# Cross-attention and mixture of experts on one core: the queries and keys stacked from SBUF to SBUF, the start of the kernel in four pieces, and 20 transposes of the identity

## The chip, the cores and the metric

The kernel is one program on one NeuronCore of a Trainium2 chip. The time is that of the device in microseconds; the kernel before took 1139.05 us (median of 3 runs, 1137.99 to 1144.78).

## The reference, cut to what matters

The input is `x` (8 batches of 256 tokens, 512 features) and a context of the same shape. One layer is computed, in float32:

```
x = x + attention(layernorm(x), ctx)      # 32 query heads of 16, 8 key/value groups
x = x + experts(layernorm(x))             # top 4 of 32 experts, a large and a small one each
```

```
qh = q @ Wq.T ;  kh = ctx @ Wk.T ;  vh = ctx @ Wv.T
score = qh @ kh / sqrt(16) ;  attn = softmax(score) ;  out = (attn @ vh) @ Wfc.T + bfc
```

Four heads share one group of keys and values. The change touches the attention alone; routing and the experts stay as they are.

## The kernel before, in words

The attention runs batch by batch (`b` of 8) and, within a batch, in 16 **steps** (`j`), each of two heads. A score is wanted at float32 accuracy from bf16 matmuls, so each of `q` and `k` is split into three bf16 parts (high, middle, low; ACT, DVE and POOL make one each: `q_first`, `q_split`, `q_third`, lines 229 to 405). The parts are then **stacked** over 96 partitions, so that one matmul with 96 rows gives the six products that count: `qst` holds high three times, middle twice, low once, `kst` the matching partners. Two more rows (96 and 97) hold the negative row maximum, so that the second score matmul gives score minus maximum.

The stacking moves data between partitions and is done by DMAs of the SP queue. Before, they go by DRAM: `store_q` writes `q3` to `qd` (L140), and `stack_q` reads it back in three DMAs of 48, 32 and 16 partitions (L151). The same holds for `k` (L157, and six DMAs of 16 partitions, L169). `stack_max` (L184) sends the two rows of maxima of one **chunk** (4 steps, 8 heads) in two DMAs.

Each step on TensorE is, in this order (L750 to L759):

```
scores(b, j)            # stp: 4 matmuls with 98 rows, exp on ACT follows; at j = 0, 4, 8, 12 waits for the chunk's maxima
side_items(b, j)        # one slice of other work: projections, transposes, the output product
scores_for_max(b1, j1)  # s: 4 matmuls with 96 rows for the step LEAD steps ahead, row maxima on DVE follow
values(b, g)            # ov: only in even steps, the products with v
```

`LEAD` is 9: the maxima run nine steps ahead. A chunk of maxima is turned by `transpose_max` (L573, out tile `turn`), which waits until DVE has reduced the chunk's last heads; `split_max` (L419) makes two bf16 parts; `stack_max` sends them. `transpose_max` stands in steps 3, 7, 11 and 15, behind a slice of other side work. As it turns the chunk that step j-1 completed, two of these steps later its scores are asked for.

The SP queue's order in batch b is: stack k and q of batch b+1 (they wait for the last scores of batch b-1, because the buffers alternate), the context of b+2, then the maxima of the chunks, and the stores of b+2. Chunk 1 of a batch is turned in step 15 of the batch before, so its DMAs are issued ahead of the stacking.

Before the loop there is a **start**: load `x`, context and weights; moments, rsqrt by ACT `Sqrt` and DVE reciprocal, normalise; project k, v, q of batch 0, then of batch 1 (L715 to L737); then nine steps of maxima of batch 0 (L739 to L746); then the loop.

Of the kernel before, what the change touches and what calls it, by code (L numbers as in the profile page):

```python
# [14 lines left out]
P = 128  # L15
# [13 lines left out]
RUNS = ((0, 3), (1, 2), (2, 1))  # L29
ROWS_QK = DH * sum(n for _, n in RUNS)  # L30
ROWS_ST = ROWS_QK + 2
LEAD = 9
CH = 4
# [5 lines left out]
def attention(nc, x_in, ctx_in, wq, wk, wv, wfc, bfc, xs, st_new, ident, qd, kd):  # L39
# [3 lines left out]
    with ExitStack() as ctx:  # L43
# [7 lines left out]
        ctxT = sb("ctxT", [P, C, S], F32)  # L51
# [3 lines left out]
        std, rstd = sb("std", [P, NT], F32), sb("rstd", [P, NT], F32)  # L55
        xn = sb("xn", [P, TT, D], F32)
        xnT = sb("xnT", [P, C, S], F32)
        q3 = sb("q3", [P, 3, C * S], BF16)
# [21 lines left out]
        kvw_loaded, wq_loaded = sem("kvw_loaded"), sem("wq_loaded")  # L80

        GROUPS = ((0, 2), (2, 4), (4, 10), (10, 16))
        x_loaded = [sem(f"x_loaded{n}") for n in range(len(GROUPS))]
        c_loaded = sem("c_loaded")
        ident_ready, set_up = sem("ident_ready"), sem("set_up")
        stats, var_ready, std_ready, rstd_ready = sem("stats"), sem("var_ready"), sem("std_ready"), sem("rstd_ready")
# [11 lines left out]
        q_stored, k_stored, q_stacked, k_stacked = sem("q_stored"), sem("k_stored"), sem("q_stacked"), sem("k_stacked")  # L98
# [4 lines left out]
        def q_parts(n):  # L103

            return [q3[:, l, n * 512:(n + 1) * 512] for l in range(3)]
# [12 lines left out]
        def _(sp):  # L118
# [6 lines left out]
            def load_ctx(b):  # L125
                sp.dma_start(ctxT[:, :, :], ctx_in[b]).then_inc(c_loaded, DMA)
# [3 lines left out]
            sp.dma_start(Wk[:, :, :], wk).then_inc(kvw_loaded, DMA)  # L130
            sp.dma_start(Wv[:, :, :], wv).then_inc(kvw_loaded, DMA)
            sp.dma_start(Wq[:, :, :], wq).then_inc(wq_loaded, DMA)
            for k in range(1, len(GROUPS)):
                load_x(k)
            sp.dma_start(Wfc[:, :, :], wfc).then_inc(w_loaded, DMA)
            sp.dma_start(Bfc[:, :], bfc).then_inc(w_loaded, DMA)

            def store_q(b):
                sp.wait_ge(q_lo, b * 2 + 2)
                sp.dma_start(qd[b].rearrange("l p n -> p l n"), q3[:, :, :]).then_inc(q_stored, DMA)  # L140

            def stack_q(b):

                sp.wait_ge(q_stored, b * DMA + DMA)
                if b >= 2:
                    sp.wait_ge(st_ready, (b - 1) * H)
                src = qd[b].rearrange("l (d g) n -> (l d) (g n)", g=G)
                at = 0
                for l, n in RUNS:
                    dst = qst[b % 2][at:at + n * DH, :, :].rearrange("p h t -> p (h t)")  # L150
                    sp.dma_start(dst, src[0:n * DH, :]).then_inc(q_stacked, DMA)  # L151
                    at += n * DH

            def store_k(b):

                sp.wait_ge(k_lo, b + 1)
                sp.dma_start(kd[b].rearrange("l p n -> p l n"), k3[b % 2][:, :, :]).then_inc(k_stored, DMA)  # L157

            def stack_k(b):

                sp.wait_ge(k_stored, b * DMA + DMA)
                if b >= 2:
                    sp.wait_ge(st_ready, (b - 1) * H)
                src = kd[b].rearrange("l (d g) n -> l d (g n)", g=G)
                at = 0
                for l, n in RUNS:
                    for _ in range(n):
                        dst = kst[b % 2][at:at + DH, :, :].rearrange("p g t -> p (g t)")
                        sp.dma_start(dst, src[l]).then_inc(k_stacked, DMA)  # L169
                        at += DH  # L170

            def next_ctx(b):
                if b < NB:
                    sp.wait_ge(v_full, b)
                    load_ctx(b)

            def stack_max(n):

                b, c = n // NC, n % NC
                sp.wait_ge(mt_empty, n + 1)  # L180
                heads = slice(c * 2 * CH, (c + 1) * 2 * CH)
                for l in range(2):
                    dst = qst[b % 2][ROWS_QK + l:ROWS_QK + l + 1, heads, :].rearrange("o h t -> o (h t)")
                    sp.dma_start(dst, nm[n % 2][:, l, :])\  # L184
                      .then_inc(m_ready[n % 2], DMA)

            sp.wait_ge(set_up, 1)
            store_k(0)
            next_ctx(1)
            stack_k(0)  # L190
            store_q(0)
            stack_q(0)
            store_k(1)
            stack_k(1)
            store_q(1)
            stack_q(1)
            for n in range(LEAD // CH):
                stack_max(n)

            for b in range(NB):  # L200
                if 0 < b < NB - 1:
                    stack_k(b + 1)
                    stack_q(b + 1)
                next_ctx(b + 2)
                for j in range(3, J, CH):
                    if chunk_at(b, j) < NB * NC:
                        stack_max(chunk_at(b, j))
                    if j == 11 and b < NB - 2:
                        store_q(b + 2)
                        store_k(b + 2)  # L210

        @block.gpsimd
        def _(pool):
# [4 lines left out]

            def add_bias(b):
# [5 lines left out]

            def q_third(b, n):

                pool.wait_ge(q_mid, b * 2 + n + 1)
                pool.tensor_tensor(q_parts(n)[2], qres[n][:, :], q_parts(n)[1], ALU.subtract).then_inc(q_lo, 1)  # L229
# [7 lines left out]
            q_third(0, 0)  # L237
            q_third(0, 1)
# [4 lines left out]
            for b in range(3):  # L243
                add_bias(b)
            for b in range(NB):
                if b < NB - 2:
                    q_third(b + 2, 0)
                if b < NB - 3:
                    add_bias(b + 3)
                if b < NB - 2:  # L250
# [4 lines left out]
        def _(act):  # L255
            def deviations(k):
                t0, t1 = GROUPS[k]
                act.wait_ge(var_ready, k + 1)
                act.activation(std[:, t0:t1], mv[:, t0:t1, 1], ACT.Sqrt, bias=eps[:, :]).then_inc(std_ready, 1)
# [5 lines left out]
            def k_first(b):  # L265
                act.wait_ge(k_full, b + 1)
                if b >= 2:
                    act.wait_ge(k_stored, (b - 1) * DMA)
                act.copy(k3[b % 2][:, 0, :], turn[:, 0:S]).then_inc(k_hi, 1)

            def v_evac(b):

                act.wait_ge(v_full, b + 1)
                if b == 0:
                    act.wait_ge(set_up, 1)
# [4 lines left out]

            def q_first(b, n):
                if n == 0 and b:
                    act.wait_ge(q_stored, b * DMA)
                act.wait_ge(qp_full, b * 2 + n + 1)
                act.copy(q_parts(n)[0], side[:, :]).then_inc(q_hi, 1)
# [25 lines left out]

            deviations(0)
            k_first(0)
            v_evac(0)
            deviations(1)
            x_evac(0, 0)
            x_evac(0, 1)
            q_first(0, 0)
            q_first(0, 1)
            deviations(2)  # L320
            deviations(3)
# [4 lines left out]
            q_first(1, 1)  # L326

            for b in range(NB):
                for j in range(J):
                    exponentials(b, j)  # L330
                    if j == 0 and b < NB - 2:
                        x_evac(b + 2, 0)
                    if j == 1 and b:
                        ov_evac(b - 1, 3)
                    if j == 1 and b < NB - 2:
                        x_evac(b + 2, 1)
                    if j == 1 and b < NB - 1:
                        v_evac(b + 1)
                    if j == 4 and b:
                        o_evac(b - 1, 0)  # L340
                    if j == 4 and b < NB - 2:
# [3 lines left out]
                    if j == 5 and b:  # L345
                        o_evac(b - 1, 1)
                    if j == 11 and b < NB - 2:
                        q_first(b + 2, 1)
                    if j == 12 and b < NB - 2:
# [6 lines left out]
        def _(dve):  # L356
            dve.memset(eps[:, :], EPS)
            for i in range(2):
                dve.memset(mx[i][:, :], 0.0)
                dve.memset(vx[i][:, :, :, DH:VW], 1.0)  # L360
                m = dve.memset(kst[i][ROWS_QK:P, :, :], 1.0)
            m.then_inc(set_up, 1)

            def moments(k):

                dve.wait_ge(x_loaded[k], DMA)
                for t in range(*GROUPS[k]):
                    dve.bn_stats(st6[:, t, :], xs[:, t, :]).then_inc(stats, 1)
                for t in range(*GROUPS[k]):
# [4 lines left out]
            def invert(k):  # L374

                t0, t1 = GROUPS[k]
                dve.wait_ge(std_ready, k + 1)
                dve.reciprocal(rstd[:, t0:t1], std[:, t0:t1]).then_inc(rstd_ready, 1)
                dve.wait_ge(rstd_ready, k + 1)
# [17 lines left out]

            def q_split(b, n):

                dve.wait_ge(q_hi, b * 2 + n + 1)  # L400
                if b:
                    dve.wait_ge(q_lo, b * 2 + n - 1)
                dve.tensor_tensor(qres[n][:, :], side[:, :], q_parts(n)[0], ALU.subtract).then_inc(qp_empty, 1)  # L403
                dve.wait_ge(qp_empty, b * 2 + n + 1)
                dve.tensor_copy(q_parts(n)[1], qres[n][:, :]).then_inc(q_mid, 1)  # L405

            def row_max(b, j):
                for r in range(2):
                    h = 2 * (j % CH) + r
                    dve.wait_ge(s1_ready, b * H + 2 * j + r + 1)  # L410
                    dve.tensor_reduce(mx[j // CH % 2][:, 2 * h:2 * h + 2], s1[r][:, :, :], AX.X, ALU.max)\  # L411
                       .then_inc(max_done, 1)

            def split_max(n):

                dve.wait_ge(mt_full, n + 1)
                if n >= 2:
                    dve.wait_ge(m_ready[n % 2], n // 2 * 2 * DMA)
# [5 lines left out]
            def weigh(b, p):  # L424
# [8 lines left out]
                dst = o[b % 2][:, :, p * P:(p + 1) * P].rearrange("p t (k d) -> p t k d", d=DH)  # L433
# [13 lines left out]
            invert(0)  # L447
# [962 lines left out]
```

## Time and profile before

| | before |
|---|---|
| median of 3 runs | 1139.05 us |
| profiled execution, its own time | 1136.86 us |
| its span | 1135.1 us |
| TensorE busy in the span | 1026.3 us, 90% |
| VectorE busy | 423.1 us, 37% |
| ScalarE busy | 347.1 us, 31% |
| GpSimd busy | 292.9 us, 26% |
| first score matmul for the exponentials | 68.18 us |

The profile page gives busy time per engine, the span in 40 slices, the DMA queues, the chain that ended last and the costliest groups. The loop of the attention runs from about 68 to 430 us, routing to about 500 us, the experts to the end.

### The profile page before, as it was taken

To read this page: it belongs to the slowest core of one execution; us is meant where nothing else is said; L and a number is where in the kernel's file an instruction comes from. 1 tells how busy PE (TensorE), PEld (TensorE's weight loads), DVE (VectorE), ACT (ScalarE), POOL (GpSimd) and SP (SyncE) were. 2 spreads that over 40 slices of the span, in tenths; PEclk is the share of its full clock that TensorE was granted. 3 is DMA by queue.
4 is the path that set the end of the run, shared out by engine and by line. 5 is a ranking of instruction groups with operands and counts; after the bars stand their busy time and mean duration, and the time that the engine had idled before them with its cause. 6 is when DMAs were issued, how large, how long until landed. Compare 5 with 4: busy or idle time off the path is not lost.

```text
span 1135.1 us, 18843 instructions
## 1 busy us (share of the span) xinstructions
PE 1026.3 (90%) x5498; PEld 660.9 (58%) x5500; DVE 423.1 (37%) x1019; ACT 347.1 (31%) x630; POOL 292.9 (26%) x381
## 2 busy tenths in 40 slices
PE   5589999999999988427999999999999999999995
PEld 4356666666655536315666666666666666666662
DVE  5457667666667624691111111111111111111110
ACT  1135544555545533141222222222222222222221
POOL 1211101101000000202344334334334343433442
PEclk9779999999999998757999999999999999999998
DMA  8531451422513003931755776675665767667433
GB/s 307 136 72 48 79 122 39 90 75 52 125 36 71 3 1 133 366 115 42 222 148 141 217 220 146 213 224 144 190 171 150 207 181 199 198 153 221 76 65 48
DMA packets 44120, 154.51 MB, mean 136 GB/s; under 512 B 9136, under 2 KB 12336, under 8 KB 38960
## 3 DMA queue, kind: packets, MB, share of 16 engines
q1 hardware_dynamic: 26448, 111.23, 31.0%
q0 software_dynamic: 17632, 42.74, 19.2%
q8 instruction: 26, 0.43, 0.2%
q14 instruction: 14, 0.11, 0.0%
HBM read 116.46 MB, written 37.22 MB: 135 GB/s over the span
## 4 chain that ended last, share of the span: by engine, by line
PE 53%; issue 1%; DMA 0%; ACT 0%; DVEq 0%; POOL 0%; DVE 0%; POOLq 0%; ACTq 0%
PE y_ps L1324 18%; PE g_ps L1307 15%; PE u_ps L1307 15%; PE xt_ps L1300 3%; PE at_ps L1316 2%; DMA xg<-xd,gidx 0%; POOL out_x L1211 0%; DVEq L1288 0%; ACT sg L1236 0%; ACT yb L1243 0%; ACT xT L1232 0%; DVE aT L1265 0%; DVEq L1289 0%; DVE a L1278 0%; DVE a L1279 0%
## 5 line engine op out<-in xcount | busy, mean ns | idle before, releaser
L1324 PE MATMUL y_ps<-W,aT 128*128 x468 | 215.5, 597 | 2.5 <-DVE aT L1265 2.5
L1211 POOL DMA_INDIRECT out_x<-yb,yidx x78 | 125.3, 1606 | 298.0 <-DMA out_x<-yb,yidx 134.7
L309 ACT ACTIVATE pt<-stp 128x512 f32<-128x512 f32 x256 | 139.0, 596 | 173.2 <-PE stp L556 172.2
L411 DVE TENSOR_REDUCE mx<-s 128x2 f32<-128x512 f32 x256 | 164.0, 682 | 69.4 <-PE s L542 68.0
L1307 PE MATMUL g_ps<-W,xT 128*128 x624 | 183.3, 437 | 0.9 <-ACT xT L1232 0.9
L1307 PE MATMUL u_ps<-W,xT 128*128 x624 | 181.3, 433 | 0.0
L1307 PEld LDWEIGHTS u_ps<-W,xT 128*128 128x128 f32 x624 | 119.1, 191 | 49.9 <-issue 0.8
L1307 PEld LDWEIGHTS g_ps<-W,xT 128*128 128x128 f32 x624 | 113.5, 192 | 39.0 <-issue 2.4
L1278 DVE TENSOR_TENSOR a<-u_ps,sg 128x192 f32<-128x192 f32 x78 | 27.9, 358 | 287.6 <-ACT sg L1236 287.6
L1324 PEld LDWEIGHTS y_ps<-W,aT 128*128 128x128 f32 x468 | 83.5, 192 | 78.3 <-issue 78.3
L1236 ACT ACTIVATE sg<-g_ps 128x320 f32<-128x320 f32 x78 | 34.1, 437 | 305.5 <-PE u_ps L1307 305.5
L1265 DVE COPY aT<-at_ps 128x384 f32<-128x384 f32 x78 | 43.5, 558 | 183.1 <-PE at_ps L1316 176.9
L1243 ACT ACTIVATE yb<-y_ps,wt 128x512 f32<-128x512 f32 x78 | 53.6, 687 | 168.5 <-PE y_ps L1324 156.0
L1197 POOL DMA_INDIRECT xg<-xd,gidx x80 | 80.7, 1008 | 69.4 <-POOL gidx L1194 65.4
L542 PE MATMUL s<-kst,qst 96*128 96x256 bf16 x512 | 83.9, 282 | 7.5 <-DVE mx L411 7.4
L556 PE MATMUL stp<-qst,kst 98*128 98x256 bf16 x512 | 78.4, 276 | 2.8 <-DMA qst<-nm 2.3
L229 POOL TENSOR_TENSOR q<-qres,q 128x512 bf16<-128x512 f32 x16 | 19.0, 1188 | 236.5 <-DVE q L405 236.5
L542 PEld LDWEIGHTS s<-kst,qst 96*128 96x128 bf16 x512 | 48.2, 99 | 49.4 <-DVE mx L411 22.9
L514 PE MATMUL side<-xnT,Wq 128*128 128x256 f32 x256 | 66.5, 394 | 5.8 <-DVE qres L403 2.9
L1194 POOL COPY gidx<-tok 128x1 uint32 (+1 forms) x80 | 58.5, 731 | 40.1 <-POOLq L799 29.6
L569 PE MATMUL ov<-pt,vx 128*32 128x256 f32 x1024 | 68.5, 385 | 0.2
L556 PEld LDWEIGHTS stp<-qst,kst 98*128 98x128 bf16 x512 | 44.6, 98 | 35.7 <-issue 28.9
(155 smaller groups left out, 932.2 us busy)
## 6 DMA issues: line engine op xcount, KB each, us to landing
W<-in_wts SPq DMA_DIRECT2D x32, 2048.0 KB, 8.4
qd<-q SPq DMA_DIRECT2D x8, 768.0 KB, 3.6
qst<-qd SPq DMA_DIRECT2D x8, 768.0 KB, 7.5
ctxT<-in_ctx SPq DMA_DIRECT2D x8, 512.0 KB, 11.6
qst<-qd SPq DMA_DIRECT2D x8, 512.0 KB, 10.1
xd<-r_xn SPq DMA_DIRECT2D x16, 256.0 KB, 2.0
out_x<-xs SPq DMA_DIRECT2D x1, 4096.0 KB, 13.9
xs<-in_x SPq DMA_DIRECT2D x2, 1536.0 KB, 13.6
```

What stands on the lines that cost most here:

```text
L309: act.activation(pt[g % 2][:, 2 * (j % 2) + r, :, :], stp[n % STP][:, :, :], ACT.Exp, scale=DH ** -0.5).then_inc(exp_done, 1)
L411: dve.tensor_reduce(mx[j // CH % 2][:, 2 * h:2 * h + 2], s1[r][:, :, :], AX.X, ALU.max)\
L514: m = pe.matmul(side[:, k * S:(k + 1) * S], Wq[:, c, (2 * n + k) * P:(2 * n + k + 1) * P], xnT[:, c, :], start=(c == 0), stop=(c == C - 1))
L542: m = pe.matmul(s1[r][:, t, :], qst[b % 2][0:ROWS_QK, 2 * j + r, t * P:(t + 1) * P], kst[b % 2][0:ROWS_QK, j // 2, :], start=True, stop=True)
L556: m = pe.matmul(stp[n % STP][:, t, :], kst[b % 2][0:ROWS_ST, j // 2, t * P:(t + 1) * P], qst[b % 2][0:ROWS_ST, 2 * j + r, :], start=True, ...
L569: m = pe.matmul(ov[c * VW:(c + 1) * VW, g % 2, :], vx[b % 2][:, t, g, :], pt[(b * G + g) % 2][:, c, t, :], start=(t == 0), stop=(t == TT - 1))
L1194: pool.tensor_copy(idx[p][:, :], tok[:, bass.ds(s, 1)]).then_inc(idx_ready, 1)
L1197: pool.indirect_dma_start(xg[p][:, :], None, xd[:, :], bass.IndirectOffsetOnAxis(idx[p][:, :], 0))\
L1211: pool.indirect_dma_start(out[:, :], bass.IndirectOffsetOnAxis(yidx[p][:, :], 0), yb[p][:, :], None, compute_op=ALU.add).then_inc(y_added, ...
L1243: act.activation(yb[p][:, :], y_ps[:, :], ACT.Copy, scale=wt[p][:, :]).then_inc(y_empty, 1)
L1307: m = pe.matmul(ps_[p][:, 0:IW], xT[p][:, c, :], W[:, bass.ds(buf, 1), (2 * c + g) * IW:(2 * c + g + 1) * IW] .rearrange("p a f -> p (a f) ...
L1324: m = pe.matmul(y_ps[:, :], aT[p][:, c, :], W[:, bass.ds(buf, 1), GW + c * D:GW + (c + 1) * D].rearrange("p a d -> p (a d)"), start=(c == ...
```

## The change

- `store_q`, `store_k` and the DRAM tensors go. `stack_q` and `stack_k` copy from SBUF to SBUF, six DMAs each, every one to 16 partitions. `q3` and `ctxT` get a second buffer.
- Batch 0's q is projected, split and stacked in four chunks (`project_q0`, `q0_first`, `q0_split`, `q0_third`, `stack_q0`), each in a PSUM tile of its own. The heads are taken in another order (`head`), so that a chunk of the projection is a chunk of four steps.
- `LEAD` is 8. `transpose_max` stands first among the side items of steps 0, 4, 8 and 12, and every other side item moves one step later. The start's maxima of batch 0 run among the projections of batch 1.
- `stack_max` takes four DMAs a chunk; in each batch chunk 1 now comes behind the stacking and the context on the SP queue.
- The moments of batches 2 to 7 are made batch by batch, in the loop from batch 3 on; rsqrt is exp(-0.5 ln) on ACT plus one Newton step (three small DVE instructions).
- Twenty transposes of the identity run on TensorE ahead of its first wait for weights.

```diff
-RUNS = ((0, 3), (1, 2), (2, 1))
+ROWS_OF_Q = ((0, 16, 32), (48, 64), (80,))
+ROWS_OF_K = ((0, 48, 80), (16, 64), (32,))
-LEAD = 9
+LEAD = 8
...
             load_x(0)
             load_ctx(0)
+            sp.dma_start(Wk[:, :, :], wk).then_inc(wk_loaded, DMA)
             sp.dma_start(Wq[:, :, :], wq).then_inc(wq_loaded, DMA)
+            sp.dma_start(Wv[:, :, :], wv).then_inc(wv_loaded, DMA)
+            load_x(1)
+            load_ctx(1)
...
+            def stack_q0(c):
+                for n, ready in ((0, q0_hi), (1, q0_mid), (2, q0_lo)):
+                    sp.wait_ge(ready, c + 1)
+                    for at in ROWS_OF_Q[n]:
+                        dst = qst[0][at:at + DH, c::C, :]
+                        sp.dma_start(dst, q0_parts(c)[n]).then_inc(q0_stacked[c], DMA)
+            def stack_q(b):
+                if b >= 2:
+                    sp.wait_ge(st_ready, (b - 1) * H)
+                for n, ready in ((0, q_hi), (1, q_mid), (2, q_lo)):
+                    sp.wait_ge(ready, q_counts(b, 1) + 1)
+                    for at in ROWS_OF_Q[n]:
+                        dst = qst[b % 2][at:at + DH, :, :].rearrange("p h t -> p (h t)")
+                        sp.dma_start(dst, q3[b % 2][:, n, :]).then_inc(q_stacked, DMA)
...
             def stack_max(n):
                 b, c = n // NC, n % NC
                 sp.wait_ge(mt_empty, n + 1)
                 for l in range(2):
+                    for t in range(TT):
+                        dst = qst[b % 2][ROWS_QK + l:ROWS_QK + l + 1, c::C, t * P:(t + 1) * P]
+                        sp.dma_start(dst, nm[n % 2][t * G:(t + 1) * G, l, :]).then_inc(m_ready[n % 2], DMA)
+            stack_k(0)
+            stack_q0(0)
+            load_x(2)
+            for c in range(1, C):
+                stack_q0(c)
             sp.dma_start(Wfc[:, :, :], wfc).then_inc(w_loaded, DMA)
             sp.dma_start(Bfc[:, :], bfc).then_inc(w_loaded, DMA)
+            load_x(3)
+            stack_max(0)
             stack_k(1)
             stack_q(1)
             for b in range(NB):
                 if 0 < b < NB - 1:
                     stack_k(b + 1)
                     stack_q(b + 1)
                 next_ctx(b + 2)
-                for j in range(3, J, CH):
+                for j in range(0, J, CH):
                     if chunk_at(b, j) < NB * NC:
                         stack_max(chunk_at(b, j))
...
             # VectorE, the start
             moments(0)
-            invert(0)
+            refine(0)
             normalise(0, 0)
             normalise(0, 1)
             k_split(0)
+            for c in range(C):
+                q0_split(c)
             moments(1)
+            refine(1)
             normalise(1, 0)
             normalise(1, 1)
+            for j in range(LEAD):
+                if j == 1:
+                    k_split(1)
+                if j == 4:
+                    split_max(0)
+                    q_split(1, 0)
+                if j == 5:
+                    moments(2)
+                if j == 7:
+                    q_split(1, 1)
+                row_max(0, j)
+            refine(2)
             normalise(2, 0)
             normalise(2, 1)
             for b in range(NB):
                 for j in range(J):
                     if j == 0 and b >= 2:
                         add_out(b - 2, 1)
+                    if j % CH == 0 and chunk_at(b, j) < NB * NC:
+                        split_max(chunk_at(b, j))
-                    if j == 2 and b:
+                    if j == 3 and b:
                         weigh(b - 1, 3)
+                    if j == 4 and b < NB - 3:
+                        moments(b + 3)
-                    if j == 5 and b < NB - 2:
+                    if j == 6 and b < NB - 2:
                         q_split(b + 2, 0)
-                    if j in (6, 10, 14):
+                    if j in (7, 11, 15):
                         weigh(b, j // 4 - 1)
-                    if j == 9 and b:
+                    if j == 10 and b:
                         add_out(b - 1, 0)
...
             # TensorE
+                if j % CH == 0 and chunk_at(b, j) < NB * NC:
+                    ...
+                    transpose_max(chunk_at(b, j))
-                if j == 5 and b:
+                if j == 6 and b:
                     pe.wait_ge(ot_empty, (b - 1) * TT + 1)
                     transpose_o(b - 1, 1)
                     if b < NB - 2:
-                        pe.wait_ge(qp_empty, (b + 2) * 2 + 1)
+                        pe.wait_ge(qp_empty, q_counts(b + 2, 0) + 1)
                     project_out(b - 1, 0, (0,))
-                if j == 9 and b < NB - 2:
+                if j == 10 and b < NB - 2:
                     if b:
                         pe.wait_ge(fc_empty, (b - 1) * TT + 1)
                     project_q(b + 2, 1, (0, 1, 2))
...
+            pe.wait_ge(ident_ready, 2)
+            for _ in range(20):
+                pe.transpose(turn[:, 0:P], ident[:, :], ident[:, :])
+            pe.wait_ge(wk_loaded, DMA)
             project_k(0)
+            transpose_x0(0)
+            transpose_x0(1)
+            pe.wait_ge(wq_loaded, DMA)
+            pe.wait_ge(xt_empty, TT)
+            for k in range(C):
+                project_q0(k)
+            pe.wait_ge(wv_loaded, DMA)
             project_v(0, 0)
             project_v(0, 1)
             project_k(1)
+            for j in range(LEAD):
+                scores_for_max(0, j)
+                if j == 0:
+                    transpose_x(1, 0)
+                if j == 1:
+                    transpose_x(1, 1)
+                if j == 2:
+                    project_q(1, 0, range(C))
+                if j == 3:
+                    project_q(1, 0, range(C, 2 * C))
+                    transpose_max(0)
+                if j == 5:
+                    project_q(1, 1, range(C))
+                if j == 6:
+                    project_q(1, 1, range(C, 2 * C))
```

## Rows read from the trace of the kernel before

**Rows 1.** The page's first part: busy time, share of the span, instructions.

```profile
PE 1026.3 (90%) x5498; PEld 660.9 (58%) x5500; DVE 423.1 (37%) x1019; ACT 347.1 (31%) x630; POOL 292.9 (26%) x381
```

**Rows 2.** Windows by stage: length, busy time per engine, granted clock, DMA share, GB/s.

```profile
0.00:68.00 68.00, 38.33 (x150) 25.43 (x151) 38.81 (x84) 9.33 (x17) 14.62 (x18) 0.81 0.71 207
68.00:107.00 39.00, 36.79 (x307) 26.71 (x311) 25.12 (x49) 20.50 (x39) 5.53 (x5) 0.93 0.12 40
107.00:380.00 273.00, 263.11 (x2163) 174.59 (x2153) 183.43 (x355) 137.45 (x263) 25.12 (x23) 1.00 0.34 73
```

**Rows 3.** Timeline of the start: start us, duration us, engine, line, instruction.

```profile
6.38 1.29 DVE L368 BATCH_NORM_STATS2 st<-xs 128x6 f32<-128x512 f32 x2
...
7.67 3.78 PE L522 MATMUL turn<-ctxT,Wk 128*128 128x256 f32 x8 [7.67 <-DMA Wv<-in_wv]
...
25.07 1.89 PE L522 MATMUL turn<-ctxT,Wk 128*128 128x256 f32 x8
...
52.35 5.46 DVE L411 TENSOR_REDUCE mx<-s 128x2 f32<-128x512 f32 x8
...
59.06 7.74 SPq L184 DMA_DIRECT2D qst<-nm  x4
...
68.18 1.01 PE L556 MATMUL stp<-qst,kst 98*128 98x256 bf16 x4 [2.33 <-DMA qst<-nm]
...
72.40 0.99 PE L556 MATMUL stp<-qst,kst 98*128 98x256 bf16 x4
...
80.14 0.60 PE L556 MATMUL stp<-qst,kst 98*128 98x256 bf16 x4
```

**Rows 4.** The page's DMA issues: times, KB each, median us from issue to landing.

```profile
Wq<-in_wq SPq DMA_DIRECT2D x1, 1024.0 KB, 7.3
```

**Rows 5.** Groups of instructions from 0 to 68 us: busy us, mean ns of one.

```profile
L411 DVE TENSOR_REDUCE mx<-s 128x2 f32<-128x512 f32 x18 | 11.6, 682 | 0.6
...
L368 DVE BATCH_NORM_STATS2 st<-xs 128x6 f32<-128x512 f32 x16 | 9.9, 677 | 0.0
...
L403 DVE TENSOR_TENSOR qres<-side,q 128x512 f32<-128x512 f32 x4 | 2.8, 691 | 20.4 <-ACT q L285 20.4
...
L378 DVE RECIPROCAL rstd<-std 128x2 f32<-128x2 f32 (+1 forms) x4 | 0.7, 169 | 1.1 <-ACT std L259 1.1
```

**Rows 6.** Timeline in batch 2, steps 3 to 5: TensorE and VectorE.

```profile
165.66 0.60 PE L542 MATMUL s<-kst,qst 96*128 96x256 bf16 x4
166.09 0.60 PE L556 MATMUL stp<-qst,kst 98*128 98x256 bf16 x4
...
168.27 0.60 PE L542 MATMUL s<-kst,qst 96*128 96x256 bf16 x4
168.80 1.07 PE L569 MATMUL ov<-pt,vx 128*32 128x256 f32 x16
```

**Rows 7.** Timeline of VectorE over the same steps.

```profile
168.69 1.29 DVE L411 TENSOR_REDUCE mx<-s 128x2 f32<-128x512 f32 x2 [1.32 <-PE s L542]
```

**Rows 8.** Waits of TensorE from 68 to 385 us: total us, times, longest us.

```profile
PE side L527 <- DVE xs L442: 6.1, 5, 1.6
...
PE turn L582 <- ACT xo L293: 1.9, 3, 0.6
PE side L514 <- DVE xs L442: 1.2, 4, 0.3
```

**Rows 9.** Timeline of the SP queue in batch 1: issues.

```profile
110.31 2.84 SPq L169 DMA_DIRECT2D kst<-kd  x6
113.24 1.30 SPq L151 DMA_DIRECT2D qst<-qd  x3
```

**Rows 10.** The tile qst, DMAs issued from 119 to 121 us (maxima of one chunk): landing.

```profile
DMA to landing us min/median/max: 6.9/7.5/8.1
```

**Rows 11.** Windows on the DMAs: k stacking, the end of a q stacking, a whole q stacking.

```profile
46.00:48.85 2.85, 2.85 (x16) 2.41 (x15) 0.00 (x0) 0.00 (x0) 0.80 (x1) 1.00 0.51 138
...
40.50:43.50 3.00, 3.00 (x11) 2.27 (x9) 0.00 (x0) 0.00 (x0) 0.00 (x0) 0.67 0.72 102
...
114.20:124.50 10.30, 10.30 (x92) 7.69 (x91) 7.08 (x14) 5.39 (x12) 0.00 (x0) 1.00 1.01 169
```

More of the change, by code:

```diff
@@ L24 @@
 DMA = 16
-RUNS = ((0, 3), (1, 2), (2, 1))
-ROWS_QK = DH * sum(n for _, n in RUNS)
+ROWS_QK = 6 * DH
 ROWS_ST = ROWS_QK + 2
-LEAD = 9
+ROWS_OF_Q = ((0, 16, 32), (48, 64), (80,))
+ROWS_OF_K = ((0, 48, 80), (16, 64), (32,))
+X_BEGINS = (0, 2, 4, 10)
+LEAD = 8
 CH = 4
@@ L50, in attention @@
         Bfc = sb("Bfc", [P, D], F32)
-        ctxT = sb("ctxT", [P, C, S], F32)
+        ctxT = [sb(f"ctxT{i}", [P, C, S], F32) for i in range(2)]
         st6 = sb("st6", [P, NT, 6], F32)
@@ L145, in stack_q, with stack_k @@
+            def stack_k(b):
                 if b >= 2:
                     sp.wait_ge(st_ready, (b - 1) * H)
[L147 to L157, printed above, removed]
@@ L217, in _ @@
                                pattern=[[-1, P]], channel_multiplier=1).then_inc(ident_ready, 1)
+            for i in range(2):
+                m = pool.memset(vx[i][:, :, :, DH:VW], 1.0)
+            m.then_inc(vx_ready, 1)
+            pool.wait_ge(vx_ready, 1)
+            for i in range(2):
+                m = pool.memset(kst[i][ROWS_QK:P, :, :], 1.0)
+            m.then_inc(kst_ready, 1)
+            pool.wait_ge(kst_ready, 1)
             def add_bias(b):
@@ L279, in v_evac, with q0_first @@
                    .then_inc(v_empty, 1)
+            def q0_first(c):
+                act.wait_ge(q0_full, c + 1)
+                act.copy(q0_parts(c)[0], q0_ps[c]).then_inc(q0_hi, 1)
             def q_first(b, n):
[L282 to L285, printed above, removed]
+                if n == 0 and b == 2:
+                    for c in range(C):
+                        act.wait_ge(q0_stacked[c], 6 * DMA)
+                elif n == 0 and b > 2:
+                    act.wait_ge(q_stacked, (b - 2) * 6 * DMA)
+                act.wait_ge(qp_full, q_counts(b, n) + 1)
+                act.copy(q_parts(b, n)[0], side[:, :]).then_inc(q_hi, 1)
             def ov_evac(b, p):
@@ L326, in _ @@
             q_first(1, 1)
+            deviations(2)
             for b in range(NB):
@@ L358, in _, with moments @@
             for i in range(2):
[L359 to L367, printed above, removed]
+                m = dve.memset(mx[i][:, :], 0.0)
+            m.then_inc(mx_clear, 1)
+            def moments(b):
+                if b * TT in X_BEGINS:
+                    dve.wait_ge(x_loaded[X_BEGINS.index(b * TT)], DMA)
+                for t in range(b * TT, b * TT + TT):
                     dve.bn_stats(st6[:, t, :], xs[:, t, :]).then_inc(stats, 1)
-                for t in range(*GROUPS[k]):
+                for t in range(b * TT, b * TT + TT):
                     dve.wait_ge(stats, t + 1)
@@ L450, in _ @@
             k_split(0)
+            for c in range(C):
+                q0_split(c)
             moments(1)
-            invert(1)
-            q_split(0, 0)
-            moments(2)
-            q_split(0, 1)
+            refine(1)
             normalise(1, 0)
             normalise(1, 1)
-            moments(3)
-            invert(2)
-            invert(3)
-            k_split(1)
-            q_split(1, 0)
-            q_split(1, 1)
+            for j in range(LEAD):
[10 more added lines that the diff above has]
+            refine(2)
             normalise(2, 0)
             normalise(2, 1)
-            for j in range(LEAD):
-                if j and j % CH == 0:
-                    split_max(j // CH - 1)
-                row_max(0, j)
             for b in range(NB):
@@ L500, in _, with transpose_x0 @@
         def _(pe):
+            def transpose_x0(t):
+                pe.wait_ge(xn_ready, t + 1)
+                for c in range(C):
+                    m = pe.transpose(x0_ps[t][:, c * P:(c + 1) * P], xn[:, t, c * P:(c + 1) * P], ident[:, :])
+                m.then_inc(xt_full, 1)
             def transpose_x(b, t):
@@ L506, in transpose_x, with project_q0 @@
                 m.then_inc(xt_full, 1)
+            def project_q0(k):
+                for c in range(C):
+                    m = pe.matmul(q0_ps[k], Wq[:, c, k * P:(k + 1) * P], xnT[:, c, :], start=(c == 0), stop=(c == C - 1))
+                m.then_inc(q0_full, 1)
             def project_q(b, n, parts):
```

347 lines of the change are left out of this document (160 added, 187 removed).

## The prediction

> **What bounds the kernel now.** I read the page's busy shares first, then windows by stage, then the timeline of the start, TensorE's waits in the loop, and last the SP queue. TensorE is busy 90% of the span [rows 1]. By stage it is busy 38.3 of the first 68 us, at a mean granted clock of 0.81, and 263 of 273 us in the loop of batches 1 to 6, at 1.00 [rows 2]. So the start is bound by a chain (project, split, store, stack, reduce) with TensorE waiting, and the loop by TensorE's own instructions: only a wait on its in-order queue can lengthen it. The waits there are few [rows 8]; that TensorE waits for no chunk of maxima in the loop comes from where `transpose_max` stands, and the change moves it.
>
> **The start, what it gains.** Before, the row maxima begin at 52.35, the loop at 68.18, its step 1 at 72.40 and step 4 at 80.14 [rows 3]. After:
> - Moments of batch 0 start at 6.4 as now; 1.6 us, then two small ACT instructions and three DVE ones of 0.17 in place of one each [rows 3, 5]: about 0.9 later than now, x normalised at 10.3, transposed and evacuated at 11.7. Wq, issued one place earlier, lands by 10 (2.76 + 7.3 now) [rows 4], so it does not hold.
> - Four chunks of q of eight matmuls, each like the second k projection, 1.89 us at full clock [rows 3]: 11.7 to 19.2. v 2.2, k of batch 1 1.9: first `scores_for_max` at 23.3. Chunk 0 is split by 15.6 and its six issues are out by 16.7: it lands by about 19 and is hidden by v and k. Chunk 1 has 1.5 MB of x ahead of it, lands near 23.5, and is not asked for until step 4 of the start.
> - VectorE is free of `q0_split` at 20.4 (the last chunk's cast, subtraction and cast, 1.3 us by half of the 0.69 us row and its like [rows 5]), then moments 1.6, Newton step with its ACT part 1.4, normalise 1.0: 24.4. From there 16 reductions at 0.682 = 10.9, k split 0.75, two q splits 2.3, maxima 0.65, moments 1.6 [rows 5] = 16.2 us, plus some 4.5 us in which it waits for projections that stand between the maxima: 45.1. Then TensorE turns chunk 1, and step 1 begins at 45.9, 26.5 us before today's 72.40.
> - In step 1 `transpose_x` waits for `split_max(1)`, which stands on VectorE behind refine and normalise of batch 2 (1.7 us). Step 4 can begin at 54.7; 1.3 us of q projection (six matmuls, steps 3 and 4 before) still lie ahead. Gain: 80.14 - 54.7 - 1.3 = **24.1 us**.
>
> The 20 transposes fill the time before the weights land. The first k projection took 3.78 us, the same instructions later 1.89 [rows 3]: TensorE had done nothing before it and ran at the lower of its two levels (1.2 and 2.4 GHz). Warm, it saves up to 1.9 us, but x is normalised only at 10.3, after either version of k is done, so on the path I count 0. Their own cost is 0: they end near 6.5, under the load. If they ended late they would cost at most 1 us. The removed table switch and the extra ln/exp are 1.3 us and 0.6 us of an idle ACT: 0.
>
> **The loop, what it loses.** Steady costs: from one s block to the next instruction 0.43, scores 0.44 more, values 1.0 [rows 6]. VectorE starts its two reductions 0.42 after the s block and needs 1.29: done 1.71 after, and TensorE sees it 0.15 later, at 1.86 [rows 6, 7].
> - (a) `transpose_max` before: in steps 3, 7, 11, 15, behind values of the even step, scores and side work, over 2.4 us after the s block: no wait. After: first side item of an even step; the step before is odd and has no values. TensorE is there 0.43 + 0.44 = 0.87 after the s block and waits until 1.86: **1.0 us**. Behind it on TensorE are all side items and the next s block, so nothing takes it up. Steps 0, 8, 12 of batches 1 to 7 (20 of them), two in batch 0, plus 0.9 there where `weigh` has no output product beside it: 22.9.
> - (b) Chunk 1. SP may start the next batch's stacking when the last scores are issued, 2.7 us before step 0. Six k issues (2.84) and six q issues at 0.43 [rows 9], then the context, then the four of chunk 1, which is now turned in step 0. DMAs of this queue land in their order: maxima issued at 119.75, in the middle of a q stacking, took 6.9 to 8.1 us [rows 10]. q data start 1.1 after step 0. Duration of the 1.5 MB: unknown for SBUF to SBUF. The k stacking, also DMAs to 16 partitions each, ran at 138 GB/s [rows 11], giving 11 us; today's q at 169 with 48, 32 and 16 partitions; its end, the 16-partition DMA, at 102, giving 14.4; nothing in the trace forbids 7 us, as its large loads are faster still. I take 11, the nearest row. Context 1.3 and chunk 0.7 more: landing 14.1 after step 0 (10.1 to 17.5). Step 4 begins at 3.1 + 2.2 + 3.5 + 2.2 = 11.0. Wait **3.1 us** (0 to 6.5), and then (a) is covered in step 4. Batches 1 to 5 15.5; batch 6 (no context) 1.8; batch 7 only (a), 1.0; batch 0 2.7 (landing 57.4 against 54.7): 21.0.
> - (c) Moved by one step, other hand-overs change parity too. Step 6: the output product needs `side` after `q_split`, at 1.71 + 0.68 + 0.1 = 2.4 after the s block; TensorE is there at 0.43 + 0.44 + 0.44 = 1.3, where it had 1.0 of values before: 1.1 x 5. Step 10: q projection after `add_out`, 2.5 against 0.87: 1.6, today 0.3 [rows 8]: 1.3 x 5. Step 2 `xnT`: 0.2 x 6. Together 13.2.
> - (d) Gone: the 6.1 and 1.9 us of waits for xs and xo [rows 8]: their consumers now stand a step later. -8.0.
>
> The moments in step 4 are 1.6 us of VectorE, the four issues a chunk 0.9 more of SP: VectorE is idle a third of the loop [rows 2], and a chunk turned in step 4 or 8 has 11 us; 0. If VectorE were late they would each show as a longer (a).
>
> Sum on the profiled execution's own 1136.9 (the median of the runs is 2.2 higher): -24.1 + 22.9 + 21.0 + 13.2 - 8.0 = +25.0, **1162**.
>
> The rule that speaks for a long stacking is the Trainium skill's, SBUF — State Buffer, section "Door 1: The DMA port swizzle": DMA bandwidth depends on how many of 16 ports the partitions reach, and 16 neighbours reach four, a quarter of 436 = 109 GB/s, an estimate of 14.4 us. By it the sum would be that of the third rival. The 102 GB/s agree, the 138 do not.
>
> **Rivals.**
> - *The stacking lands in time.* If SBUF as source makes 1.5 MB take 7 us, (b) is only 7 x 1.0: 1148. For it: no store and no DRAM read; against it: the destination rows are the same few partitions. Chance 0.20.
> - *Faster: the hand-overs (a) and (c) stay covered.* Place: steps 0, 6, 8, 10, 12. It decides at a wait under 0.1 us where I count 1.0: VectorE would have to be through the reductions 0.9 us sooner after the s block than row and rule of order say. Then -24.1 + 21.0 - 8.0 = -11, 1126; with (b) short as well 1112. For it: only the gain at the start is sure, and TensorE's waits may overlap one another. Against: VectorE's row [rows 7]. Chance 0.17.
> - *Stacking held by the destination.* 14.4 us: waits of 6.5 for 3.1 in seven batches, +24: 1186. For it the 102 GB/s. Chance 0.12.
> - The start gains less: gaps on TensorE lower the granted clock as between 0 and 68 now [rows 2]; four q projections at half speed, +7: 1169. Within the range.
>
> **Numbers.** Forecast 0.51, with the last point in it. 1% is about what can be told from no change: 1127.7 and 1150.4 bound it. Faster 0.17 (second rival), same 0.24 (first rival and the low end of the forecast), slower 0.59. The range leaves out the lower half of the second and the upper end of the third rival: 1122 to 1184.
>
> **What would show it.** First scores of the loop near 42.6 and step 1 near 46; TensorE's waits for `mx` at L575's successor some 25 times at 1 us; waits of stp for qst<-nm six or seven times at 2 to 6 us; q stacking of 11 us; side waiting for qres and xs five times each. It is wrong if the chunks' waits are missing, or if the loop from step 4 of batch 0 to the last output takes no longer than now.

## The result, and the profile after

| | before | after |
|---|---|---|
| median | 1138.5 us (1135.0 to 1144.8, 4 runs) | 1199.9 us (1197.5 to 1203.4, 4 runs) |
| span of the profiled execution | 1135.1 us | 1199.7 us |
| ratio of the times | | 1.0535, 95% interval 1.048 to 1.059 |

The kernel is 5.4% slower. The direction was forecast, the size was not: the range ended at 1184. The page of after, its busy line (before: [rows 1]) and granted clock in 40 slices:

```profile
PE 1039.2 (87%) x5518; PEld 670.4 (56%) x5520; DVE 425.5 (35%) x1039; ACT 348.7 (29%) x643; POOL 297.2 (25%) x387
...
PEclk9898989898989899985799999999999999999997
```

TensorE has 12.9 us more busy time. Of these 4.4 are the 20 transposes, the only instructions it has more by count; the rest goes with the lower clock. It dips in every second slice of the attention, where the page of before has 9 in each slice from 85 us to the end of the attention. The windows of after, to be read beside [rows 2] (columns as there):

```profile
0.00:68.00 68.00, 53.51 (x329) 42.03 (x331) 42.05 (x93) 21.26 (x45) 14.68 (x21) 0.92 0.72 186
68.00:107.00 39.00, 28.17 (x255) 19.53 (x254) 21.78 (x45) 15.60 (x30) 4.29 (x4) 0.93 0.44 65
107.00:380.00 273.00, 216.87 (x1641) 143.41 (x1642) 149.15 (x298) 105.60 (x207) 22.96 (x21) 0.92 0.25 38
```

In the first window TensorE is busy 15 us more (4.4 of them with the 20 transposes); in the third, inside the loop, 46 us less, and the clock there fell from 1.00 to 0.92. Waits of TensorE from 0 to 520 us, after (total us, times, longest), to be read beside [rows 8]:

```profile
PE stp L625 <- DMA qst<-nm: 54.6, 8, 9.3
PE turn L647 <- DVE mx L459: 20.3, 23, 1.2
PE side L580 <- DVE xs L490: 6.6, 5, 1.3
...
PE side L667 <- DVE qres L451: 4.4, 5, 0.9
```

These are the waits that the forecast named. The first is nearly three times as large. In the profiled executions all of the lost time lies before the routing: its first transposes come at 494.2 us in place of 429.6, 64.6 us later, and from there to the end both kernels take 705.5 us. Timeline of the start, after (beside [rows 3]):

```profile
1.59 4.37 PE L777 MATMUL turn<-ident 128*128 128x128 f32 x20 [1.59 <-POOL ident L224]
...
6.14 1.99 PE L588 MATMUL turn<-ctxT,Wk 128*128 128x256 f32 x8 [0.18 <-DMA Wk<-in_wk]
...
6.91 1.00 DVE L424 TENSOR_SCALAR xn<-xs,mv,rstd 128x512 f32<-128x512 f32 x2
...
42.87 0.71 PE L625 MATMUL stp<-qst,kst 98*128 98x256 bf16 x4 [3.33 <-DMA qst<-nm]
...
44.44 1.06 PE L625 MATMUL stp<-qst,kst 98*128 98x256 bf16 x4
...
56.45 0.61 PE L625 MATMUL stp<-qst,kst 98*128 98x256 bf16 x4 [1.38 <-DMA qst<-nm]
```

Step 4 begins at 56.45 in place of 80.14: the start won what was forecast. Then one batch of the loop, on TensorE (steps 0, 3, 4 and 5, and step 0 of the next batch) and on the SP queue, the latter to be read beside [rows 9]:

```profile
148.99 0.60 PE L625 MATMUL stp<-qst,kst 98*128 98x256 bf16 x4
150.41 0.30 PE L647 MATMUL turn<-ident,mx 128*128 128x128 f32 x1 [0.82 <-DVE mx L459]
...
159.35 0.60 PE L611 MATMUL s<-kst,qst 96*128 96x256 bf16 x4
167.59 1.04 PE L625 MATMUL stp<-qst,kst 98*128 98x256 bf16 x4 [7.63 <-DMA qst<-nm]
...
168.63 2.77 PE L580 MATMUL side<-xnT,Wq 128*128 128x256 f32 x6
...
174.41 1.46 PE L580 MATMUL side<-xnT,Wq 128*128 128x256 f32 x6
...
209.24 0.60 PE L625 MATMUL stp<-qst,kst 98*128 98x256 bf16 x4
```

```profile
146.59 3.82 SPq L165 DMA_DIRECT2D kst<-k  x6
150.52 4.81 SPq L183 DMA_DIRECT2D qst<-q  x6
155.38 0.59 SPq L147 DMA_DIRECT2D ctxT<-in_ctx  x1
156.01 44.49 SPq L197 DMA_DIRECT2D qst<-nm  x16
```

The sixteen issues of the last row are four chunks; its first four, chunk 1, are issued from 156.0 to 158.8 and the chunk is there at 167.4. In the trace the packets of the q stacking run from 151.6 to 165.3: 1.57 MB in 13.7 us, 115 GB/s. During the wait and behind it the clock is at the lower of the two levels, 1.2 GHz, though TensorE is full again by 170 (windows of 4 us, after):

```profile
162.00:166.00 4.00, 0.00 (x0) 0.00 (x0) 0.00 (x0) 0.00 (x0) 0.00 (x0) 0.59 1.02 167
166.00:170.00 4.00, 2.41 (x9) 1.96 (x10) 1.09 (x4) 1.08 (x2) 0.00 (x0) 0.50 0.08 27
170.00:174.00 4.00, 4.00 (x29) 2.16 (x28) 2.17 (x6) 0.05 (x1) 0.00 (x0) 0.63 0.01 2
```

Two groups of the same six matmuls of the q projection show it: 2.77 us at 168.63, 1.46 at 174.41. A batch, from step 0 to step 0, lasts about 60 us, where it lasted 46.

### The profile page after: what moved, and what is told of

It reads as the page before. It is cut to its first block, busy times and chain, and to the rows that moved or that the text cites. A ratio compares the mean times of both kernels' runs of the same rounds, so it can differ in the third digit from the quotient of the medians.

```text
span 1199.7 us, 19018 instructions
## 1 busy us (share of the span) xinstructions
PE 1039.2 (87%) x5518; PEld 670.4 (56%) x5520; DVE 425.5 (35%) x1039; ACT 348.7 (29%) x643; POOL 297.2 (25%) x387
## 4 chain that ended last, share of the span: by engine, by line
PE 50%; issue 0%; DMA 0%; POOL 0%; ACT 0%; DVE 0%; POOLq 0%; ACTq 0%
PE y_ps L1390 17%; PE g_ps L1373 14%; PE u_ps L1373 14%; PE xt_ps L1366 3%; PE at_ps L1382 2%; DMA xg<-xd,gidx 0%; POOL out_x L1277 0%; ACT yb L1309 0%; ACT xT L1298 0%; DVE aT L1331 0%; ACT sg L1302 0%; DVE a L1344 0%; DVE a L1345 0%; POOL gidx L1260 0%; ACTq L1308 0%
## 5 line engine op out<-in xcount | busy, mean ns | idle before, releaser
L625 PE MATMUL stp<-qst,kst 98*128 98x256 bf16 x512 | 81.4, 283 | 54.8 <-DMA qst<-nm 54.6
L252 POOL TENSOR_TENSOR q<-qres,q 128x512 bf16<-128x512 f32 x14 | 16.2, 1156 | 315.0 <-DVE q L453 315.0
L641 PE MATMUL ov<-pt,vx 128*32 128x256 f32 x1024 | 71.1, 397 | 0.2
L580 PE MATMUL side<-xnT,Wq 128*128 128x256 f32 x224 | 62.8, 420 | 6.7 <-DVE xs L490 6.6
```

Source lines behind the costliest of these rows:

```text
L580: m = pe.matmul(side[:, k * S:(k + 1) * S], Wq[:, c, (2 * n + k) * P:(2 * n + k + 1) * P], xnT[:, c, :], start=(c == 0), stop=(c == C - 1))
L625: m = pe.matmul(stp[n % STP][:, t, :], kst[b % 2][0:ROWS_ST, head(j, r) // C, t * P:(t + 1) * P], qst[b % 2][0:ROWS_ST, head(j, r), :], st ...
L641: m = pe.matmul(ov[c * VW:(c + 1) * VW, g % 2, :], vx[b % 2][:, t, g % 2 * C + c, :], pt[(b * G + g) % 2][:, c, t, :], start=(t == 0), sto ...
```

## The experiments

Each is the changed kernel with the edit shown, compared with the kernel before on the same chip. There the kernel before took 1137.7 to 1138.8 us each time, and 1138.5 beside after, so the times are also set against after's 1199.9.

**The 20 transposes taken out.**

```diff
-            for _ in range(20):
-                pe.transpose(turn[:, 0:P], ident[:, :], ident[:, :])
```

> The 20 transposes of the identity are left out, all else as in the changed kernel (1199.9 us). If they are off the path, as the prediction had it: first k projection 3.8 us instead of 1.99, and the time the same within 3 us, because x is normalised at 7.9 in the changed kernel and the k projection then ends at 9.9. Rival: the lower clock reaches into the transposes of x and the projection of q, which are on the path now: the loop starts 2 to 5 us later, time 1202 to 1205.

Measured: 1204.9 us, ratio 1.0594 (1.0558 to 1.0629). The median lies 5.0 us above after's, where the rival had put it, but the intervals overlap, and the spans of the profiled executions are 1198.7 and 1199.7. The timeline of this kernel:

```profile
6.95 3.75 PE L588 MATMUL turn<-ctxT,Wk 128*128 128x256 f32 x8 [6.95 <-DMA Wk<-in_wk]
...
44.62 0.60 PE L625 MATMUL stp<-qst,kst 98*128 98x256 bf16 x4 [3.20 <-DMA qst<-nm]
```

Its k projection ends 2.6 us later, of which 0.8 is a later landing of the weights; step 0 begins 1.75 us later. The routing begins at 494.9 in place of 494.2. The transposes are worth 1 to 2 us of the start, and nothing that the total can show.

**Chunk 1 sent ahead of the stacking.**

```diff
             for b in range(NB):
+                if b:
+                    stack_max(chunk_at(b, 0))
                 if 0 < b < NB - 1:
                     stack_k(b + 1)
                     stack_q(b + 1)
                 next_ctx(b + 2)
-                for j in range(0, J, CH):
+                for j in range(CH if b else 0, J, CH):
```

> In batches 1 to 7 the SP queue sends the maxima of chunk 1 before it stacks k and q of the next batch; nothing else changes. Theory (the maxima stand behind 2.5 MB of stacking and context in the queue, and TensorE's waits of 54.6 us in all, 8 of them, are this): the waits for the maxima fall to under 8 us, the granted clock in the loop goes back to 1.00, and the time falls by 50 (waits) + 12 to 16 (clock): 1135 to 1150. The stacking then ends some 8 us later in the batch, about when its first use in step 8 comes: a wait of 0 to 3 us per batch there may take the place, then up to 1165. Rival (the maxima are late because they are turned late, in step 0): the waits stay above 40 us, time above 1190.

Measured: 1166.4 us, ratio 1.0258 (1.0228 to 1.0288), 33.5 us less than after. TensorE's waits and one chunk, in this kernel:

```profile
PE stp L627 <- DMA qst<-nm: 25.6, 8, 6.0
PE turn L649 <- DVE mx L461: 20.7, 23, 1.2
```

```profile
168.48 0.61 PE L627 MATMUL stp<-qst,kst 98*128 98x256 bf16 x4 [2.27 <-DMA qst<-nm]
```

In batches 1 to 6 step 4 waits no longer. The wait in this row is step 8's, for chunk 2, which is now the one behind the stacking: part of the wait only moved. Both the theory (waits under 8 us, at most 1165) and the rival (above 40) missed. Of the 25.6 us 7.7 are waits of batch 0, which the edit does not touch, and the six of step 8 are 17.9, where step 4 had 49.9.

**The stacked rows six apart.** Row d of part n goes to partition 6d + n (for q and k alike) instead of 16n + d, so a DMA to 16 partitions reaches over 96. The sum over rows does not change.

```diff
-                        dst = qst[b % 2][at:at + DH, :, :].rearrange("p h t -> p (h t)")
+                        dst = qst[b % 2][at // DH:ROWS_QK:6, :, :].rearrange("p h t -> p (h t)")
```

> Only the rows of the stack change: each part of q and k goes to every sixth of the 96 partitions instead of 16 neighbouring ones (same bytes, same number of DMAs, same matmuls up to the order of the summed rows). Theory (16 neighbouring destination partitions hold the stacking at 115 GB/s, 13.7 us for 1.5 MB of q): the stacking of q takes 5 to 8 us of data time instead of 13.7, the waits for the maxima fall from 54.6 to under 20 us, time 1140 to 1165. Rival (the reading of SBUF in rows of 2 KB, or the issuing by SP at 0.64 us per DMA, holds it): data time stays above 12 us, time above 1190.

Measured: 1160.1 us, ratio 1.022 (1.0157 to 1.0283), 39.8 us less than after. The tile qst, the six DMAs of one q stacking, from issue to landing, first after, then this kernel:

```profile
DMA to landing us min/median/max: 5.8/9.2/11.6
```

```profile
DMA to landing us min/median/max: 3.8/4.9/6.7
```

```profile
PE turn L647 <- DVE mx L459: 22.0, 25, 1.2
PE stp L625 <- DMA qst<-nm: 15.5, 7, 3.0
```

The q stacking took 8.5 us (147.1 to 155.6), 185 GB/s, with the same bytes and the same number of DMAs. So what was slow was where the data went, not that they came from SBUF. What is left, up to 3.0 us a batch, is the chunk's place in the queue, still behind thirteen issues of about 0.6 us and their data; the last experiment below takes it away.

**TensorE kept busy in the wait.**

```diff
+                if j == 4 and 0 < b < NB - 1:
+                    pe.wait_ge(ovt_empty, b * C)
+                    for _ in range(64):
+                        pe.transpose(turn[:, 0:P], ident[:, :], ident[:, :])
```

> In batches 1 to 6, 64 transposes of the identity into the tile turn run on TensorE ahead of the scores of step 4, that is in the wait for the maxima; they do no work that is used. If the lower granted clock after each wait (10.2 us at half in each batch) costs what its rows say, about 2.6 us for each of six batches, the time falls by 12 to 16 us, to 1184 to 1188, with the waits themselves shorter only by the time the transposes take and the granted clock 1.00 in the loop. Rival (the clock costs nothing because TensorE then waits for others): 1200, unchanged, or up to 1206 if the transposes end after the maxima land.

Measured: 1191.7 us, ratio 1.0474 (1.0447 to 1.05), 8.2 us less than after, less than I expected. Window, waits, and rows of one batch:

```profile
107.00:380.00 273.00, 243.81 (x1962) 171.97 (x1961) 153.04 (x306) 109.18 (x214) 24.09 (x22) 0.99 0.26 40
```

```profile
PE stp L629 <- DMA qst<-nm: 13.0, 8, 3.0
```

```profile
162.56 7.15 PE L620 MATMUL turn<-ident 128*128 128x128 f32 x64
170.97 0.61 PE L629 MATMUL stp<-qst,kst 98*128 98x256 bf16 x4 [1.26 <-DMA qst<-nm]
...
171.53 1.46 PE L580 MATMUL side<-xnT,Wq 128*128 128x256 f32 x6
...
210.08 0.60 PE L629 MATMUL stp<-qst,kst 98*128 98x256 bf16 x4
```

The maxima come as late as in after: from the scores of step 0 to those of step 4 batches 1 to 6 take 114.4 us in all, in after 114.3. Behind step 4 the work is the same and faster: from its scores to step 0 of the next batch it takes 39.11 us in the batch shown, in after 41.65 (167.59 to 209.24), and over the six batches 227.2 in place of 239.5. That is 12.3 us less, as I expected; batch 0, which the edit does not touch, took 3.4 us longer in this execution, and the routing begins 9.3 us sooner. In batch 1 nothing was won, as the clock fell there once more. Against 39.11 in batches 1 to 5 and 30.01 in batch 6, the lengths at full clock, after loses 13.9 us behind its six waits. So the low clock costs some 14 us on top of the waits, by the rows; the medians show 8.2 of it.

**The maxima turned at the end of the step**, `transpose_max` behind the next s block and values, `split_max` behind `row_max`; once alone, once with the rows apart.

```diff
 # TensorE, step j: scores, side items, scores_for_max, values
+                    turn_maxima(b, j)
 # VectorE, step j
                     if b1 < NB:
                         row_max(b1, j1)
+                    if j % CH == 0 and chunk_at(b, j) < NB * NC:
+                        split_max(chunk_at(b, j))
```

> The transposes of the maxima move from the first side item of steps 0, 4, 8 and 12 to behind the maxima's matmuls and the values of the same step, and the split of the maxima on VectorE behind that step's reductions. Theory (each transpose waits for reductions that were only just given their input, 20.3 us in 23 waits): these waits vanish, the waits for the chunks of maxima stay (the queue holds them, not the turn), time 1176 to 1184. Rival (the wait only moves, to the next step's transposes of x behind the split): 1195 to 1200.

> Rows of the stack six apart (1160.1 alone) and the transposes of the maxima late in their step. If the two waits are separate and add: 1160 less 18 to 22, so 1138 to 1142. If they cover one another (a later turn makes the maxima later by 2 us where they are already waited for, 15.5 us in 7 waits): 1146 to 1155.

Measured: alone 1196.0 us, ratio 1.0505 (1.0474 to 1.0536), 4 us less than after; with the rows apart 1151.7 us, 1.0126 (1.0104 to 1.0147), 8.4 less than with the rows apart alone. Waits of the first:

```profile
PE stp L625 <- DMA qst<-nm: 50.9, 8, 8.8
PE turn L565 <- DVE nm L469: 8.1, 6, 4.2
PE s L611 <- DVE mx L459: 7.6, 22, 1.9
```

The 20.3 us for mx at L647 are gone, and most of them came back: the next `transpose_x` now waits 8.1 us for `split_max` (0.7 in after), transposes in two other lines 3.0, and the next s block 7.6 for the reductions, in place of 3.5. Alone it is the rival that came true, with the rows apart the range for waits that cover one another. Moving one instruction in this loop mostly moved its wait.

**The loop in the order of before, with the start and the stacking of after.** LEAD 9, maxima turned in steps 3, 7, 11 and 15, chunk 1 ahead of the stacking, side items where they were; once with neighbouring rows, once with rows six apart.

```diff
-LEAD = 8
+LEAD = 9
             stack_max(0)
             stack_k(1)
+            stack_max(1)
             stack_q(1)
-                for j in range(0, J, CH):
+                for j in range(3, J, CH):
...
-                if j % CH == 0 and chunk_at(b, j) < NB * NC:
-                    ...
-                    transpose_max(chunk_at(b, j))
+                if j == 7:
+                    if b:
+                        project_out(b - 1, 0, (2,))
+                    pe.wait_ge(ovt_empty, b * C + 1)
+                    transpose_max(chunk_at(b, j))
```

> The changed kernel's start and its stacking from SBUF to SBUF, with the loop of the kernel before: LEAD 9, its order of side items on TensorE, VectorE and ScalarE, chunk 1 of the maxima sent ahead of the stacking; moments and Newton steps of later batches stay in the loop, steps 4 and 7. Theory (the start gains 22 to 24 us and all of the loss is the order of the loop and the queue): 1138.8 - 22 to 24 = 1113 to 1118, waits for the maxima in the loop under 3 us. Rival (the stacking from SBUF at 115 GB/s costs the loop by itself): some waits of the stacked q or of chunk 2 in steps 7 and 8, 1120 to 1140.

> As the run before it, with rows six apart. If the stacking's data time is hidden in that loop: within 4 us of it, faster by 1 to 3 us at the start of the loop at most. If it is not hidden: faster by the waits that run shows.

> The best version again, with more rounds: the changed kernel's start and its stacking SBUF to SBUF, the loop in the order of the kernel before, stacked rows six apart. The first comparison gave 1114.9 against 1135, ratio 0.982 with an interval of 0.977 to 0.987. Theory: the gain of the start (some 21 us) is all there is, and the loop costs what it did before; 1113 to 1117, ratio 0.979 to 0.984. Rival: the first comparison was lucky by some us and the direct stacking costs the loop 3 us or more: ratio 0.985 to 0.99.

Measured: neighbouring rows 1125.9 us, ratio 0.988 (0.9861 to 0.99); rows six apart 1114.9, 0.9819 (0.977 to 0.9867), and again with more rounds 1113.6, **0.9774 (0.9759 to 0.979)**. That version beats both kernels. TensorE's waits from 60 to 480 us with neighbouring rows:

```profile
PE side L596 <- DVE xs L491: 6.1, 5, 1.6
...
PE stp L628 <- DMA qst<-nm: 3.8, 6, 0.9
PE turn L657 <- ACT xo L324: 3.4, 5, 0.8
PE s L614 <- issue: 3.3, 2, 2.4
PE s L614 <- DVE mx L460: 2.9, 9, 0.9
```

With neighbouring rows the rival came true (1120 to 1140), not the theory. With rows six apart the waits for nm and those named issue are gone and the others stay. They make 7.1 of the 11 us between the two; the other 4 were not traced further. So the stacking's data time was not hidden in this loop.

**Rows six apart and chunk 1 first, in the new loop.** Both edits above together.

> The changed kernel with both mends of its own loop: stacked rows six apart (as in the earlier run, 1160.1) and chunk 1 sent ahead of the stacking in batches 1 to 7. The question is what the loop's order costs when neither the speed of the stacking nor its place in the queue is against it. Theory (queue): the 15.5 us of waits for the maxima that were left with rows six apart are chunk 1 behind 13 issues of about 0.6 us. Sent first, it is there in time; chunk 2, issued some 9 us later, still meets q data, but these take 8.5 us in place of 13.8, so less than 4 us of waits stay. Some of the 22 us for mx come back into view. Expected 1147 to 1151, and what stays above the old loop with rows six apart (1114.9) is some 33 us: mx 22, xs and qres 11. Rival (the waits only change place, as with the chunk first and neighbouring rows, where 25.6 us stayed): chunk 2 waits 2 us in each batch, 1156 to 1160, no gain over rows six apart alone.

Measured: 1144.6 us, ratio 1.0049 (1.003 to 1.0068). Waits from 0 to 480 us:

```profile
PE turn L649 <- DVE mx L461: 26.8, 31, 1.2
...
PE side L582 <- DVE xs L492: 6.6, 5, 1.3
...
PE side L669 <- DVE qres L453: 4.4, 5, 0.9
...
PE stp L627 <- DMA qst<-nm: 1.8, 1, 1.8
```

That is 2.4 us below the range. This is the new loop without its waits for the queue. TensorE waits for mx 31 times; after has 23 of these waits, the others being covered there by waits for chunks. The five for xs and the five for qres are as in after.

## Why the prediction was wrong, by its own steps

The two chains of edits take the change apart in medians. Before to the start and stacking alone (rows apart): -24.1 (1137.7 to 1113.6). From there to the new order of the loop, chunk 1 first: +31.0 (to 1144.6). From there to the change as it is: +55.3 (to 1199.9). They add up to +62.2; measured +61.4. By the begin of the routing in the profiled executions (429.6, 410.9, 442.8 and 494.2) the same steps are -18.7, +31.9 and +51.4, so that up to 5 us of the -24.1 lie outside the attention and in the spread of the runs; that it equals the forecast of the start is chance.

- **The start: right in size, by errors that cancelled.** -24.1 forecast. Step 4 at 56.45, with 1.3 of projection ahead, is 22.4 less than before, against 21.4 forecast with its wait. Inside, x was normalised at 7.9, not 10.3, as its first tiles landed at 4.2; with that the k projection was on the path after all, so the transposes did 1 to 2 us where I counted 0. And chunk 0 was not hidden: 3.3 us of wait in step 0.
- **(a) and (c): right.** 22.9 forecast for mx, 20.3 measured (26.8 with the queue's waits away); 13.2 more forecast for xs, qres and the like, 9.8 measured (qres 4.4; xs 6.6, less the 1.2 that before had at the same place). Without (b), (a) + (c) - (d) was +28.1; the middle step of the chain gave +31.0. The rival in which these hand-overs stay covered fell. (d): 8.0 forecast, 8.7 measured (xs 6.1; xo 0.8 in place of 3.4).
- **(b): the failed step.** Six batches were to wait 17.3 us in all and waited 49.9 (54.6 less the 3.3 and 1.4 of the start), 8.3 each in place of 2.9 (3.1, in batch 6 1.8). In batch 2, TensorE came to step 4 at 11.0 after step 0, as forecast. Chunk 1 landed at 18.4 in place of 14.1. Of these 4.3 us, 2.7 are the duration of the q stacking: I took 11 us from the k stacking at 138 GB/s [rows 11] as the nearest row, where the 102 GB/s of the last, 16-partition DMA, 14.4 us, came closer to the 13.7 measured. 1.5 are that q's data began 2.6 and not 1.1 after step 0: I took 0.47 and 0.43 us for each issue from [rows 9], and the six of k, now from SBUF to SBUF, took 0.64 each, 1.0 us more; SP also began 2.4 and not 2.7 before step 0. The trace of before had a nearer price: its 64 DMAs of maxima, from SBUF to SBUF, held the queue for 0.58 us in the median. Over the six batches the waits were 7.6 to 9.3; what varies between them was not traced further. That both causes are real is shown: rows apart alone leaves 15.5 us, chunk first alone 25.6, both 1.8.
- **The clock: missing.** I priced a lower clock at the start only. Each wait of 8 us in the loop was followed by matmuls at half clock, 13.9 us in all by the rows; the run that kept TensorE busy gave 12.3 of it back in its rows and 8.2 in its median. It does not stand in any row of before, where no wait in the loop was over 1.6 us [rows 8], but it could have been bounded by the windows of the start [rows 2].
- **The sum.** +25.0 forecast. (b) +32.6, the clock +13.9, (a) and (c) -6.0, (d) -0.7 and the start -1.0 give +63.8. The profiled executions, from which all of these are taken, differ by 64.6; the medians differ by 61.4. That only 0.8 is left is in part luck, as smaller waits were not priced one by one.

The third rival was the nearest: the destination did hold the stacking, though 1186 was still 14 too low. In the runs the same bytes took 13.7 us to neighbouring rows and 8.5 to rows six apart. The Trainium skill, SBUF — State Buffer, section "Door 1: The DMA port swizzle", says that bandwidth depends on how many of the 16 ports the partitions reach, and gives four for 16 neighbours, 109 GB/s. The 115 GB/s agree within 6%. Rows six apart reach 13 or 14 ports by the page's mapping; the gain to 185 GB/s agrees in direction, but it is a factor of 1.6 where the ports are more than three times as many, and what holds it at 185 no run shows. I gave the rival 0.12 because one row of the trace, the 138 GB/s of k, seemed to speak against it.

## What to carry to other kernels

In a loop that its in-order TensorE bounds, price a reordering by each hand-over whose distance it shortens, and ask of every small DMA what stands before it in its queue: here 8 KB that were needed soon stood behind 2.5 MB that were needed a batch later. When a stacking DMA goes to few partitions, spread them: a stride of six in the rows was worth 40 us in this loop and 11 in the old one. Take up a change of many parts in parts; here a good start (some 22 us) was hidden by a loop order that, with neighbouring rows, cost 74 (1125.9 to 1199.9).

## What the runs showed of the hardware

- Copies of 256 KB from SBUF to 16 neighbouring partitions ran at 115 GB/s in a train of six, to 16 partitions six apart at 185 GB/s (batch 2 of after and of the run with rows apart).
- A stacking DMA from SBUF to SBUF held the SP queue for 0.60 us in the median (after, 48 of k and 42 of q), one that read the stack back from DRAM for 0.42 (before, 48 of k and 24 of q). It is not the source alone: the context, from DRAM, took 0.59 to 0.66 where it stood right behind the stacking.
- After a wait of TensorE of 7.6 us the granted clock was at 1.2 GHz, in the batch shown until 172.9, which is 5.3 us after TensorE had taken up work. From 107 to 380 us the mean clock was 0.92 with waits of 7.6 to 9.3 us, 0.97 with rows apart (waits up to 3.0) and 1.00 with rows apart and chunk 1 first, where no such wait stood.
